# Spare transposes on TensorE at four waits of the first two attention batches

## What is computed

```
x = x + attention(layernorm(x))      # 16 heads, dk 16, dv 64, per batch of 256 tokens
x = x + experts(layernorm(x))        # 32 experts of width 64, top 8 of 32, plus a shared one
x = x + band_mix(layernorm(x))       # 32 softmax taps along a sequence of 512
x = x + experts(layernorm(x))        # the same weights again
```

```
q, k, v = l2norm(q), l2norm(k), l2norm(v)
attn = square(relu(einsum('bhid,bhjd->bhij', q, k)))
out = tanh_norm(einsum('bhij,bhjd->bhid', attn, v)) @ Wout
```

## Time and profile before

| | |
|---|---|
| runs | 559.16, 559.18, 560.94 us |
| median | 559.18 us |
| the profiled execution | 555.02 us |
| its span, first to last instruction | 553.2 us |
| mean granted TensorE clock | 0.990 |
| busy: TensorE | 527.1 us (95%) |
| busy: VectorE, ScalarE, GpSimd | 425.2, 372.1, 331.7 us |

### The profile page before, as it was taken

The page is one execution under the profiler, slowest core; times in us unless marked ns, Lnnn a source line. Parts: engine busy times, 40 slices in busy tenths (PEclk is TensorE's granted clock), DMA queues, the critical chain, the costliest instruction groups (busy, mean ns, idle before and its releaser), DMA issues. The chain is left out here.

```text
span 553.2 us, 10182 instructions
## 1 busy us (share of the span) xinstructions
PE 527.1 (95%) x3288; PEld 394.6 (71%) x3288; DVE 425.2 (77%) x1004; ACT 372.1 (67%) x682; POOL 331.7 (60%) x280
## 2 busy tenths in 40 slices
PE   8798899999999997898999999999999999999997
PEld 7465557676766665686877878877877878878884
DVE  5877768788979688559769769769769768777664
ACT  5697858677879775464466875865865865855654
POOL 6645919394956564285456755755755755665563
PEclk9899989999999999999999999999999999999999
DMA  7401010101010103900192570670670680671920
GB/s 215 132 2 30 1 30 1 31 1 30 2 31 1 30 2 91 225 10 2 38 218 55 159 155 26 157 157 25 162 158 20 156 179 26 174 154 34 240 57 20
DMA packets 37253, 44.75 MB, mean 81 GB/s; under 512 B 5840, under 2 KB 20304, under 8 KB 37200
## 3 DMA queue, kind: packets, MB, share of 16 engines
q1 hardware_dynamic: 32512, 42.40, 32.3%
q10 hardware_dynamic: 4688, 1.71, 1.3%
HBM read 40.94 MB, written 3.15 MB: 80 GB/s over the span
## 5 line engine op out<-in xcount | busy, mean ns | idle before, releaser
L512 POOL TENSOR_TENSOR hl<-hb,hh 128x512 fp32r<-128x512 f32 x127 | 164.4, 1296 | 127.8 <-ACT hh L727 122.3
L720 ACT ACTIVATE sil<-PS 128x512 f32<-128x512 f32 (+1 forms) x136 | 81.0, 595 | 79.3 <-PE PS L1241 75.2
L1108 DVE TENSOR_TENSOR PS<-sil,PS 128x512 f32<-128x512 f32 x128 | 88.3, 690 | 55.5 <-PE PS L1241 33.5
L1241 PE MATMUL PS<-fxh,wfh 128*128 128x512 f32 x264 | 104.4, 396 | 3.5 <-DVE hb L1113 1.9
L1241 PE MATMUL PS<-fxl,wfh 128*128 128x512 f32 x264 | 104.0, 394 | 0.0
L1241 PE MATMUL PS<-fxh,wfl 128*128 128x512 f32 x264 | 103.8, 393 | 0.0
L727 ACT ACTIVATE hh<-hb 128x512 fp32r<-128x512 f32 x128 | 80.3, 628 | 33.7 <-DVE hb L1113 32.9
L1113 DVE TENSOR_TENSOR hb<-PS,wbc 128x512 f32<-128x512 f32 x128 | 88.4, 691 | 10.8 <-issue 3.2
L886 DVE SCALAR_TENSOR_TENSOR aT<-PS,rl 128x1024 f32<-128x1024 f32 x64 | 75.1, 1216 | 15.6 <-ACT rl L578 15.3
L578 ACT ACTIVATE rl<-PS 128x1024 f32<-128x1024 f32 x64 | 62.8, 1050 | 24.1 <-PE PS L1241 24.1
L432 POOL TENSOR_TENSOR sr<-n2o,half 128x32 f32<-128x32 f32 x7 | 38.0, 5422 | 49.2 <-DVE n2o L893 49.2
(11 more groups left out here) (182 smaller groups left out, 901.6 us busy)
## 6 DMA issues: line engine op xcount, KB each, us to landing
wbc<-w_dram SPq DMA_DIRECT2D x48, 512.0 KB, 11.6
wbc<-w_dram SPq DMA_DIRECT2D x32, 128.0 KB, 3.0
wbc<-w_dram SPq DMA_DIRECT2D x16, 256.0 KB, 4.2
wfs<-wf_dram SPq DMA_DIRECT2D x32, 98.0 KB, 2.2
band_dram<-zero SPq DMA_DIRECT2D x16, 80.0 KB, 1.7
band<-band_dram ACTq DMA_DIRECT2D x4, 320.0 KB, 3.1
X<-x_dram SPq DMA_DIRECT2D x1, 896.0 KB, 8.4
Osb<-wa_dram SPq DMA_DIRECT2D x3, 256.0 KB, 3.6
```

What stands on the lines that cost most here:

```text
L512: g.tensor_tensor(hl[:, n % RING, :], hb[:, n % RING, :], hh[:, n % RING, :].bitcast(F32), ALU.subtract).then_inc(F("hl"), 1)
L720: s.activation(sil[0:rows, n % 2, :], PS[0:rows, G0 + n % 2, :], ACT.Silu).then_inc(F("silu"), 1)
L1108: v_.tensor_tensor(PS[:, bank, :], sil[:, n % 2, :], PS[:, bank, :], ALU.mult).then_inc(F("t"), 1)
L1241: return nc.tensor.matmul(o, w, m, start=start, stop=stop)
```

## The change

A new helper issues transposes of the identity, as keep_busy does, but into the bank of the job named, and it waits first until the former user of that bank is done. It is called in four places: 6 transposes ahead of score(0), 10 ahead of score(1), 8 ahead of score(5), 10 ahead of score(9). They signal nothing, nothing reads them, and the job that owns the bank overwrites them.

```diff
+            def fill_idle(times, *job):
+                bank, k = turns.at[job]
+                after(pe, Z(f"free{bank}"), k - 1)
+                for _ in range(times):
+                    nc.tensor.transpose(PS[:, bank, 0:P], ident[:, :], ident[:, :])
+
...
             group(0, 0)
             group(0, 1)
+            fill_idle(6, "g", 0, 2)
             score(0)
...
                 more, last_batch = n < B, b == B - 1
+                if b < 2:
+                    fill_idle(10 if b == 0 else 8, "qk", n, 0)
                 if b != 2:
                     score(NG * b + 1)
...
                 if b == 1:
+                    fill_idle(10, "F", q, 0)
                     score(NG * n + 1)
                 if b:
                     spread_factors(q, 0)
```

## The result

The change makes the kernel faster by 0.59%: ratio 0.9941, 95% interval 0.9919 to 0.9962. The 22 runs of the kernel before include the three from which the prediction started.

A forecast was written before the change was run, and what follows sets the result against it. TensorE bounds the kernel, with two stretches at half clock; 0.85 - 0.04 - 0.23 + 2.12 = 2.70 us off the profiled 555.02 gives 552.3, plus 4.16 carried over gives a median of 556.5 us, range 555.3 to 559.6.

The forecast's parts named there:

- What bounds: TensorE, at half clock for 3.4 us from 20.05 and 6.8 us from 67.83; time taken from its list reaches the end.
- 0.216 us each: Length of each added transpose, read from the opening 20; 6, 10, 8 and 10 of them last 1.30, 2.16, 1.73, 2.16 us.
- The delays of 0.04 and 0.23 us: Added transposes end after the waits they fill: score(1) 0.04 us late, score(9) 0.23 us late.
- First slow stretch: Score(1) and six wide matmuls at full clock; attend(0) at 23.14 instead of 23.99, capped by GpSimd: gain 0.85 us.
- Second slow stretch: From score(9) at full clock: 0.34 ahead of the wide matmuls, 1.27 in them, 0.51 in attend(8): gain 2.12 us.
- Fill 3: Eight transposes ahead of score(5) make it 0.09 us late, 0.05 us of it covered: loss 0.04 us.
- The sum: Whole kernel: 0.85 - 0.04 - 0.23 + 2.12 = 2.70 us gained, 552.3 us against the profiled 555.02.
- From the sum to the median: Whole kernel: the median 559.18 lies 4.16 us above the profiled execution, carried over unchanged, giving 556.5 us.
- Rival 2: Slow stretches differ in timed runs: gain 0.6 or 1.85 us; chance 0.20 below 1.7 us, 0.10 for about 1.85.
- What is late next: Waits of 0.7 us at attend(0), 0.5 at factor transposes, 0.8 at spread_factors' second half; no new fall expected.
- Rival 1: Transposes don't hold the clock; falls at 20.05 and 67.83 stay, only delays remain: median 559.5 us; chance 0.12.
- Rival 3: Transposes ahead of score(1) or score(9) run at half clock, 0.43 us each: median 563.7 or about 560.7; chance 0.08.

The follow-up runs named there:

- e8: Kernel before plus the change, 38 transposes at 211 to 222 us and 26 more at 22, 68 and 251 us: median 553.03 us, ratio 0.9911.
- e11: The change without its transposes ahead of score(0) and score(5), against the kernel before: median 554.10 us, ratio 0.9947.
- e12: Same kernel as e8, timed again beside other kernels against the kernel before: median 553.08 us, ratio 0.9940.
- e2: The changed kernel run again without edit, against the kernel before: median 553.45 us, ratio 0.9927.
- e4: The change with each fill twice as long (12, 20, 16, 20 transposes), against the kernel before: median 553.68 us, ratio 0.9950.
- e3: The change plus 38 transposes in the last batch and ahead of the first experts (211 to 222 us), against the kernel before: median 553.13 us, ratio 0.9930.
- e7: The kernel before with only 38 transposes between 209 and 222 us, none of the change: median 556.4 us, ratio 0.9966.
- e5: The kernel before with only the 10 transposes ahead of score(1): ratio 0.9980 (0.9946 to 1.0014), not separated from before.
- e6: The kernel before with only the 10 transposes ahead of score(9): median 552.73 us, ratio 0.9918.
- e10: The kernel before, no edit, one execution for another trace; its own time is not given.
- e14, e15, e13: The kernel before, no edit, one execution for another trace; among the long executions near 559 us, its own time is not given.
- e1: The kernel before run again without edit, against itself: ratio 0.9991 (0.9955 to 1.0027); its trace 555.18 us.

## Why the prediction was right or wrong

**What bounds.** Right: the score, the wide matmuls and the attends in the two stretches got their full speed back, and the shift passed unshrunk through 150 us of attention, 3.38 us at 72.6 and 3.38 at 221.8. "Reaches the end" was too much. In the three traces without any fall (e8, e11, e12) the experts start 3.33, 3.38 and 3.53 us earlier than in the first trace, and the spans are 2.4, 2.0 and 2.9 us shorter. One place of the loss can be seen, in the changed kernel (first two rows) against the kernel before (third row):

```profile
409.96 3.04 ACTq L750 DMA_DIRECT2D band_dram<-wS  x4
413.74 0.50 PE L1241 MATMUL PS<-fxh,wfh 128*128 128x512 f32 x1 [0.75 <-ACT sil L720]
409.12 1.80 ACTq L750 DMA_DIRECT2D band_dram<-wS  x4
```

ScalarE took 3.04 us to issue four transfers instead of 1.80, and TensorE stood 0.75 us for its next result, at full clock. Such an issue of 2.8 to 3.1 us with a wait of 0.5 to 0.8 us stands in five of the ten traces of kernels with fills (changed, e2, e4, e8, e11), and in none of the eight of the kernel before, where the longest issue is 2.23 us. Two more, e3 and e7, have one of 2.62 and 2.49 us with a short wait; e5 and e6, with 10 added transposes each, and e12 have none. What brings it about is not shown.

**The transposes' duration.** Wrong, and not seen as wrong: "0.216 us each" was read from the opening 20. That is the half-clock time. The granted clock of the page and of the windows is 1.00 there only because no change is recorded before the first one, at 6.39 us; up to then the engine ran at half speed, and the same instruction takes 0.11 us afterwards. The opening shows it too: in e12 the clock rises at 4.21 us already, and the same 20 transposes end sooner, after 3.72 us instead of 4.53:

```profile
1.47 3.72 PE L1384 MATMUL PS<-ident 128*128 128x128 f32 x20 [1.47 <-POOL ident L398]
```

Two terms hung on it. The delays of 0.04 and 0.23 us did not come: score(9) is earlier by 67.24 - 66.35 = 0.89, the whole first gain. And the fills covered half of each wait, not all.

**First slow stretch.** Right to the hundredth: gain 23.99 - 23.13 = 0.86 against 0.85, with GpSimd's v as the cap. That there was such a stretch to win back belongs to the traces compared: three of the eight of the kernel before (e10, e14, e15) don't have it.

**Second slow stretch.** From the start of score(9) to the values behind attend(8) it took 75.97 - 67.24 = 8.73 us and takes 72.59 - 66.35 = 6.24: gain 2.49 against 2.12. The six wide matmuls gave 2.86 - (70.72 - 69.16) = 1.30 (forecast 1.27), the attend 0.52 (0.51). The part ahead of them was mis-sized: OTs can start 1.37 us after the score (67.72 in the trace) instead of the 1.59 that I put together, and the part is worth 0.67, not 0.34. Of this 0.56 is the earlier OTs; the rest is the second half of spread_factors, which also ran faster and to which the prediction gave nothing.

**Fill 3.** Costed at 0.04 and worth nothing either way (e6 and e11 do without it).

**The sum.** 3.38 against 2.70 within the attention, and 3.3 us in the ratio of many runs. That these agree is partly luck, since the ratio also holds what changed at the third and fourth places and what was lost behind 221.8 us.

**From the sum to the median: the step that failed.** "The median of the runs, 559.18, is 4.16 above it; I carry that over unchanged." The 4.16 us was not an overhead around the execution. It was two more stretches at half clock, about 10 us in all, in the upper group of executions: at 225 and 260 us (e13 to e15). Two things follow. The true median before was 557.6, not 559.2, in the larger sample, since three runs had come from one group. And the upper group all but went with the change. Before, 47 of 92 executions had a clock of 0.986 or less, where the first two stretches alone make 0.990. With those two gone, some 10 us at half speed would still bring a run down to 0.991, and only one of 34 of the changed kernel is there, at 0.989: the one traced first. From the lower group's 555.2 (e1) the sum gives 552.5, and the changed kernel's runs without a fall average 552.3.

**Rival 2, the stretches are not the same in the timed runs,** was right as a mechanism; the spread of the three runs and their distance from the trace were the signs to follow. But I priced it only as less gain, never as stretches at places where my one trace showed none. "What is late next" named three waits that were all short, and expected no new fall from them; in e2 the clock fell behind one of them, the 0.83 us for OTs. It also looked only inside the first 76 us, though the same view of waits would have shown 1.58, 1.23 and 1.70 us at 214 to 225 us, and 1.85 us at 256 in the experts.

**Rival 1, transposes don't hold the clock,** falls. In 14 of 18 traces the clock rose before 7.1 us (the earliest at 4.2), when TensorE had done nothing but transposes since 1.47 us; and in e8 and e12 transposes alone filled the waits behind which it fell otherwise. The trace thus disagrees with the sentence of the Trainium skill on PE-mode transposes (TensorE: Matmul & The Clock Gate, Part 4) as far as these fp32 transposes go. The prediction was right to give this rival a small chance, but by luck: its evidence, four microseconds of opening transposes at 1.00, was time at half speed.

**Rival 3, a fill at half clock,** did not occur in any of the traces of kernels with fills.

**What stays open.** Why the third and fourth places together take some 10 us of full clock in half of the executions before and seldom after, while TensorE's waits there are the same. Falls there did not end with the change: of the five traces with fill 4 and the third place unfilled (changed, e2, e4, e6, e11) three have one, of 10.2, 3.4 and 3.4 us. Fill 4 seems to matter most. With it and the third place unfilled, 5 of 68 runs (the changed kernel 1 of 34, e4 2 of 12, e6 2 of 10, e11 0 of 12) have a clock as low as 8 us or more at half speed behind the attention would make it; without it, 43 of 92 of the kernel before (0.983 or less) and 5 of 12 in e5 (0.985 or less) do. Between e5 and e6 alone, 5 of 12 against 2 of 10, nothing is decided. The table above shows that the first rise comes at another moment each time (4.5 to 7.2 us), and that the second stretch shifts all that follows by whole waits; that the long stretches at 66 to 76 us thereby decide whether the clock falls later is argued, not shown. e10 and e14 rise at 4.92 and 5.03 us and end in different groups.

## What to carry to other kernels

A TensorE-bound kernel can differ by 1% between executions, as this one does, because the clock falls in some and not in others. Before a sum is set against a median, look at the mean clock of every run, not at one trace; list the waits of the whole span, also short ones close together, whether or not this trace lost the clock there. Unread transposes into a bank whose reader is done are a cheap cover, not a free one. The 98 of e8 and e12 bring the spread from 7 to 2 us, but their mean of 553.0 us is hardly below the 553.2 of fill 4 alone, with 10 transposes, and where the clock stays up the changed kernel, with 34, is 0.7 us faster.

## What the runs showed of the hardware

- The granted clock before its first recorded change reads 1.00, but the same transposes take 0.216 us there and 0.11 us later: the engine starts at half speed.
- The first rise comes 4.2 to 7.5 us after the first instruction, at another moment in each execution of the same program; each stretch at half speed between this rise and the last matmuls lasted 3.4, 6.8 or 10.2 us.
- In the eight traces of the kernel before, the clock fell behind the wait of 2.1 us (score(1)) in five and around the end of the wait of 1.9 us (score(9)) in all eight. In e10 it stayed up at the first of the two and fell at the second. In e2 it fell behind waits of 0.49, 0.83 and 0.83 us close together.
- A score that lies wholly at half speed takes 2.09 us instead of 1.15 (score(9) in e14 and e15), norms 1.94 instead of 1.07 (e13), six wide matmuls 2.86 instead of 1.56 (batch 1, before and changed). The 1.85 us of score(1) and the 2.46 us of attend(8) in the first trace are mixtures, since the clock changes within them.
- ScalarE's issue of four transfers (L750, four times in each trace) took 1.8 to 2.2 us as a rule; in seven of the ten traces with fills one of the four took 2.5 to 3.1 us.
